# Last layer of a two-layer transformer on one core: half of the expert outputs kept on chip and turned by TensorE, half sent through DRAM as before

## The reference

```
grouped  = x.reshape(b, s // 32, 32, 256)               # groups n of 32 tokens: 128 in all
logits   = einsum('bntd,des->bntes', grouped, Wc) + bc   # 32 experts x 4 sets = 128 slots "es"
perm     = (logits + tie == max over the 32 tokens)      # one-hot: the token that slot es takes from group n
permuted = einsum('bntd,bntes->bnesd', grouped, perm)
inner    = relu(einsum('bnesd,esdf->bnesf', permuted, W1) + b1)    # f = 32 inner channels
result_p = einsum('bnesf,esdf->bnesd', inner, W2) + b2             # the second product
result   = einsum('bnesd,bntes->bntd', result_p, perm)             # back to the tokens
x        = x + result
```

## Time and profile before

| | us |
|---|---|
| median of three runs | 1857.89 |
| the profiled execution: its time | 1849.57 |
| the profiled execution: first to last instruction (span) | 1847.8 |
| TensorE busy | 1707.3 (92%) |
| VectorE busy | 1286.2 (70%) |
| ScalarE busy | 1145.3 (62%) |
| GpSimd busy | 821.8 (44%) |

### The profile page before, as it was taken

One profiled execution on the slowest core, in us unless ns is written; L12 is line 12 of the kernel. 1 busy time (PEld: TensorE's weight loads), 2 busy tenths in 40 slices (PEclk: granted clock), 3 DMA queues, 4 the chain that ended last, 5 costly groups with the idle time before them and its releaser, 6 DMA issues.

```text
span 1847.8 us, 41058 instructions
## 1 busy us (share of the span) xinstructions
PE 1707.3 (92%) x15760; PEld 1443.4 (78%) x15760; DVE 1286.2 (70%) x2770; ACT 1145.3 (62%) x2882; POOL 821.8 (44%) x1292
## 2 busy tenths in 40 slices
PE   5799999999999999999999789999999999988648
PEld 4567676679899999999999668888888888867523
DVE  4799998453518888888886687777777777667321
ACT  1477777423357777777775577777777777734210
POOL 2235442110103333333330677888888887644000
PEclk7799999999999999999999899999999999999766
DMA  7756565256966666666676522222223221112799
GB/s 185 212 125 137 131 128 130 72 181 223 317 232 223 242 242 240 242 243 240 244 237 239 193 71 64 69 88 72 66 64 92 70 64 54 43 49 94 267 365 325
DMA packets 140163, 303.81 MB, mean 164 GB/s; under 512 B 14080, under 2 KB 82944, under 8 KB 124736
## 3 DMA queue, kind: packets, MB, share of 16 engines
q1 hardware_dynamic: 116032, 188.68, 33.1%
q0 software_dynamic: 19584, 108.31, 17.2%
q10 hardware_dynamic: 4352, 4.20, 0.7%
HBM read 210.44 MB, written 90.44 MB: 163 GB/s over the span
## 4 chain that ended last, share of the span: by engine, by line
PE 74%; DVE 9%; DMA 7%; POOL 4%; issue 4%; ACT 1%; SPq 1%; DVEq 0%; POOLq 0%; ACTq 0%
PE ps L1250 12%; PE ps L1236 11%; PE ps L1832 5%; PE ps L373 5%; PE ps L219 4%; PE ps L1863 4%; PE ps L1818 4%; PE ps L1852 4%; PE ps L379 3%; PE ps L464 3%; PE ps L440 2%; DMA R<-rp_scratch 2%; DVE NM L592 2%; DMA rp_scratch<-RP 2%; POOL P L209 2%
## 5 line engine op out<-in xcount | busy, mean ns | idle before, releaser
L196 ACT ACTIVATE P<-ps,NM 128x256 f32<-128x256 f32 x512 | 236.2, 481 | 127.5 <-DVE NM L185 127.4
L209 POOL TENSOR_TENSOR P<-P,RS 128x1024 f32<-128x1024 f32 x128 | 242.9, 1903 | 72.5 <-DVE RS L203 72.0
L1236 PE MATMUL ps<-XRP,W1P 128*128 128x256 f32 x1872 | 226.8, 281 | 3.3 <-DVE W1P L1319 3.3
L1236 PEld LDWEIGHTS ps<-XRP,W1P 128*128 128x128 f32 x1872 | 220.1, 190 | 3.6 <-DVE W1P L1319 3.6
L1250 PE MATMUL ps<-W2P,HP 128*128 128x256 f32 x1872 | 221.5, 277 | 0.0
L1250 PEld LDWEIGHTS ps<-W2P,HP 128*128 128x128 f32 x1872 | 218.0, 188 | 0.0
L592 DVE TENSOR_REDUCE NM<-ps 128x2 f32<-128x512 f32 x256 | 164.3, 684 | 35.9 <-PE ps L440 35.1
L690 ACT ACTIVATE PT<-ps 128x512 f32<-128x512 f32 x256 | 139.2, 597 | 67.9 <-PE ps L452 65.4
L185 DVE TENSOR_REDUCE NM<-ps 128x2 f32<-128x512 f32 x256 | 164.5, 684 | 5.8 <-PE ps L1818 4.2
L1170 POOL DMA_INDIRECT WE<-in_we,WIX x39 | 44.6, 1144 | 268.9 <-DVE W1P L1319 208.8
L1279 ACT ACTIVATE HF<-ps,WE 128x256 f32<-128x256 f32 x312 | 129.0, 465 | 43.2 <-PE ps L1236 43.2
(11 more groups left out here) (225 smaller groups left out, 3688.7 us busy)
## 6 DMA issues: line engine op xcount, KB each, us to landing
KS<-k_scratch SPq DMA_DIRECT2D x64, 256.0 KB, 3.1
V<-v_scratch SPq DMA_DIRECT2D x16, 1024.0 KB, 6.3
rp_scratch<-RP SPq DMA_DIRECT2D x16, 1024.0 KB, 8.7
R<-rp_scratch SPq DMA_DIRECT2D x16, 1024.0 KB, 14.0
k_scratch<-KVM SPq DMA_DIRECT2D x52, 256.0 KB, 4.1
QS<-q_scratch SPq DMA_DIRECT2D x96, 128.0 KB, 4.5
v_scratch<-KVM SPq DMA_DIRECT2D x40, 256.0 KB, 3.0
ys_scratch<-YS SPq DMA_DIRECT2D x39, 256.0 KB, 8.1
```

The lines of the kernel that those rows point to most:

```text
L196: i = e.activation(self.P[u % 4][:, c, :], PS[SB[n % 3]][:, y * 256:y * 256 + 256], ACT.Exp, bias=self.NM[:, u % 4, c:c + 1], accum_out=se ...
L209: e.tensor_tensor(p, p, self.RS[:, u % 4, :].unsqueeze(2).to_broadcast([128, 4, 256]), ALU.mult).then_inc(self.s_pn, 1)
L1236: m = e.matmul(PS[p][:, hh * 256:hh * 256 + 256], W1P[i % 2][wi][:, cc * 1024 + hc * 128:cc * 1024 + hc * 128 + 128], XRP[i % 2][xi][:, cc ...
```

## The change

The 16 `down` steps become 8 pairs. `down_a(k)` is the second product for batches 0 to 7 (groups 0 to 63) and four experts: sixteen matmuls with 32 x 64 stationary and 256 columns moving. It is copied into `RPA` (two buffers) and goes through DRAM as before: 8 transfers of 1 MB, and 8 back. `down_b(k)` is the second product for batches 8 to 15 with the operands exchanged: the stationary operand is 32 x 128 of `WF2P`, the moving one 32 x 64 of `INT`, 32 matmuls for four experts. Channels are then on the partitions; DVE and ACT copy the banks into `RPB`, 64 KB per partition, in which the writes of one instruction are 512 bytes apart.

`turn_b(i)` turns `RPB` for one batch by 16 PE transposes into four banks, and DVE adds the bias `B2` while it moves them into `R2B` (two buffers). `back("b", ...)` needs no bias matmuls; `bias(b)` and `back("a", ...)` are the two parts of the former `back`. The returns alternate, b ahead of a (`RET`). Output transfers move from ACT's queue to SP's, in the order of `RET` and behind the `back_in` of the batch three later (`NR` = 3). `WF1P` has four buffers (6 loads in place of 8), `WF2P` four (no reuse), and the four parts of the first product in half 1 are made in the order 2, 3, 0, 1, ahead of all `down` steps.

```diff
-NR = 6
+NR = 3
+    R2A = [Arena(nc, q1_at + 8192 * i)(f"R2A{i}", [128, 8, 256], fp32) for i in range(NR)]
+    R2B = [Arena(nc, w1o_at + 8192 * i)(f"R2B{i}", [128, 8, 256], fp32) for i in range(2)]
+    RPA = [Arena(nc, ot1_at + 8192 * i)(f"RPA{i}", [128, 2, 4, 256], fp32) for i in range(2)]
+    RPB = Arena(nc, attn_at)("RPB", [128, 2, 64, 128], fp32)
+    PARTS = ((0, 1, 2, 3), (2, 3, 0, 1))
+    RET = [x for i in range(10) for x in ((("b", i - 1),) if 1 <= i <= 8 else ()) + ((("a", i - 2),) if i >= 2 else ())]
+    def rpa_free(w, k):
+        if k >= 2:
+            w.wait_ge(d_ks_rp[(k - 2) % 4], ks_sent + 16 * ((k - 2) // 4 + 1))
+    def rpb_part(k, r):
+        es = 16 * (4 * (k % 2) + k // 2) + r
+        return (RPB[:, :, :, :].rearrange("p a g s -> p s (a g)")[:, es:es + 13:4, :],
+                PS[GATHER[r]][:, :].rearrange("p (q n) -> p q n", q=4))
...
+        def down_a(k):
+            w.wait_ge(s_e0, 2 * k - 1)
+            w.wait_ge(s_e1, 2 * k - 1)
+            for h in range(2):
+                for a in range(2):
+                    for r in range(4):
+                        rows = slice(32 * r, 32 * r + 32)
+                        m = e.matmul(PS[SMALL[r]][64 * a:64 * a + 64, h * 256:h * 256 + 256],
+                                     INT[rows, 16 * a + 2 * k + h, 0:64],
+                                     WF2P[k // 2][rows, 4 * a + 2 * (k % 2) + h, :], start=True, stop=True)
+        def down_b(k):
+            w.wait_ge(s_in, 16)
+            w.wait_ge(s_e0, 2 * k)
+            w.wait_ge(s_e1, 2 * k)
+            for ql in range(4):
+                for dh in range(2):
+                    for r in range(4):
+                        rows = slice(32 * r, 32 * r + 32)
+                        c0 = (2 * ql + dh) * 64
+                        m = e.matmul(PS[GATHER[r]][:, c0:c0 + 64], WF2P[k // 2][rows, 4 * (k % 2) + ql, dh * 128:dh * 128 + 128],
+                                     INT[rows, 16 * (k % 2) + 4 * (k // 2) + ql, 64:128], start=True, stop=True)
+        def turn_b(i):
+            for t in range(4):
+                w.wait_ge(s_e0, 16 + 4 * (i - 1) + t + 1 if i else 16)
+                for u in range(2):
+                    for dh in range(2):
+                        c0 = u * 256 + dh * 128
+                        m = e.transpose(PS[SMALL[t]][:, c0:c0 + 128], RPB[:, dh, 8 * i + 2 * t + u, :], ident)
+                m.then_inc(s_fm, 1)
...
+        for x in range(4):
+            pe_up(e, w, 1, x)
+        for k in range(8):
+            down_a(k)
+            down_b(k)
+        for i in range(10):
+            if i < 8:
+                turn_b(i)
+            if i >= 2:
+                bias(i - 2)
+            if 1 <= i <= 8:
+                back("b", i - 1)
+            if i >= 2:
+                back("a", i - 2)
... dve_tail
+                for t in range(4):
+                    w.wait_ge(s_fm, 16 + 4 * i + t + 1)
+                    e.tensor_tensor(R2B[i % 2][:, 2 * t:2 * t + 2, :], PS[SMALL[t]][:, :].rearrange("p (n d) -> p n d", n=2),
+                                    B2[:, :].unsqueeze(1).to_broadcast([128, 2, 256]), ALU.add).then_inc(s_e0, 1)
... sp_tail
+        for j in range(4):
+            w.wait_ge(d_ks_rp[j], ks_sent + 16 * 2)
+        w.wait_ge(s_fm, 16)
+        for b in range(NR):
+            back_in(b)
+        for kind, b in RET:
+            if kind == "a" and b + NR < 8:
+                back_in(b + NR)
+            out(kind, b)
```

More of the change, by code:

```diff
@@ L81, in build @@
     vd = nc.dram_tensor("v_scratch", (16, 128, 2048), fp32).ap()
-    rpd = nc.dram_tensor("rp_scratch", (128, 128, 256), fp32).ap()
+    rpd = nc.dram_tensor("rp_scratch", (64, 128, 256), fp32).ap()
     X = keep("X", [128, 32, 256], fp32)
@@ L1475, in build @@
     WF2P = [Arena(nc, x3_at)("WF2P0", [128, 8, 256], fp32)]
+    XO = [Arena(nc, x3_at + 2048 * i)(f"XO{i}", [128, 2, 256], fp32) for i in range(4)]
     PMT = Arena(nc, w1q_at)("PMT", [128, 4096], f32r)
@@ L1478, in build @@
     X3P = [[mem_t(f"X3P{i}{j}", [128, 2, 256], f32r) for j in range(2)] for i in range(2)]
-    WF2P.append(Arena(nc, q1_at)("WF2P1", [128, 8, 256], fp32))
+    WF2P += [Arena(nc, q1_at + 8192 * i)(f"WF2P{i + 1}", [128, 8, 256], fp32) for i in range(3)]
+    R2A = [Arena(nc, q1_at + 8192 * i)(f"R2A{i}", [128, 8, 256], fp32) for i in range(NR)]
     WF1P = [mem_t(f"WF1P{i}", [128, 2, 32, 32], fp32) for i in range(2)]
@@ L1485, in build @@
     INT = Arena(nc, w1o_at)("INT", [128, 32, 128], fp32)
[L1486 to L1494, removed]
+    R2B = [Arena(nc, w1o_at + 8192 * i)(f"R2B{i}", [128, 8, 256], fp32) for i in range(2)]
+    WF1P += [Arena(nc, ot1_at + 8192 * i)(f"WF1P{i + 2}", [128, 2, 32, 32], fp32) for i in range(2)]
+    RPA = [Arena(nc, ot1_at + 8192 * i)(f"RPA{i}", [128, 2, 4, 256], fp32) for i in range(2)]
+    PX = Arena(nc, attn_at)("PX", [128, 2, 128, 64], fp32)
+    RPB = Arena(nc, attn_at)("RPB", [128, 2, 64, 128], fp32)
     d_c1 = sem("d_c1")
+    d_wf1, d_wf2 = [sem(f"d_wf1{i}") for i in range(2)], [sem(f"d_wf2{i}") for i in range(2)]
     wt_sent, kl_sent = 16, 16 * 32
@@ L1580, in pe_step, with pe_up @@
             gather(n - 3)
-    def pe_up(e, w, hf, j):
-        w.wait_ge(d_kl_wf1[j % 2], kl_sent + 16 * (2 * hf + j // 2 + 1))
+    def pe_up(e, w, hf, x):
+        j = PARTS[hf][x]
+        buf = j + 2 if hf and j < 2 else j % 2
+        if buf < 2:
+            w.wait_ge(d_kl_wf1[buf], kl_sent + 16 * (j // 2 + 1))
+        else:
+            w.wait_ge(d_wf1[j], 16)
         w.wait_ge(s_px, 24 * (hf + 1))
@@ L1588, in pe_up @@
                 for r in range(4):
-                    m = e.matmul(PS[GATHER[j]][32 * r:32 * r + 32, q * 64:q * 64 + 64], WF1P[j % 2][:, cc, 4 * q + r, :],
+                    m = e.matmul(PS[GATHER[j]][32 * r:32 * r + 32, q * 64:q * 64 + 64], WF1P[buf][:, cc, 4 * q + r, :],
                                  PX[:, cc, 32 * j + 4 * q + r, :], start=(cc == 0), stop=(cc == 1))
@@ L1593, in pe_tail, with second_in @@
     def pe_tail(e, w):
-        def down(q2):
-            w.wait_ge(d_wt_wf2[q2 // 4 % 2], wt_sent + 16 * (q2 // 8 + 1))
-            w.wait_ge(s_in, 8 + 2 * (q2 // 4) + 2)
+        def second_in(j):
+            if j < 2:
+                w.wait_ge(d_wt_wf2[j], wt_sent + 16)
+            else:
+                w.wait_ge(d_wf2[j - 2], 16)
+        def down_a(k):
+            second_in(k // 2)
+            w.wait_ge(s_in, 8)
             w.wait_ge(s_rb, 32)
@@ L1600, in down @@
             w.wait_ge(s_pb, 16)
[L1601 to L1608, removed]
@@ L1628, in back @@
-            m.then_inc(s_cm2, 1)
[L1630 to L1637, removed]
+                    e.matmul(M[:, lt * 256:lt * 256 + 256], PMT[:, tok + lt * 128:tok + lt * 128 + 128], B2S[j][:, :],
+                             start=(lt == 0 and j == 0), stop=(j == 1), skip_group_check=True)
+        def back(kind, b):
+            n = returned(kind, b)
+            M, tok = PS[GATHER[(n - 1) % 4]], 256 * (b + 8 * (kind == "b"))
+            if kind == "a":
+                R = R2A[b % NR]
+                w.wait_ge(d_r2[b % NR], 16 * (b // NR + 1))
+            else:
+                R = R2B[b % 2]
+                w.wait_ge(s_e0, 16 + 4 * b + 4)
+                w.wait_ge(s_xo, n - 4)
+            for lt in range(2):
+                for g in range(4):
+                    c0 = tok + lt * 128 + 32 * g
+                    m = e.matmul(M[32 * g:32 * g + 32, lt * 256:lt * 256 + 256], PMT[:, c0:c0 + 32].bitcast(fp32),
+                                 R[:, 2 * g + lt, :], start=(kind == "b" and lt == 0), stop=True, skip_group_check=True)
+            m.then_inc(s_cm2, 1)
@@ L1705, in dve_up, with r2b_free @@
         e.tensor_scalar(INT[:, 8 * j:8 * j + 8, hf * 64:hf * 64 + 64], RL[:, :, :], 0.0, None, ALU.max).then_inc(s_in, 1)
[L1707 to L1712, removed]
-    def dve_tail(e, w):
[L1715 to L1719, removed]
+    def r2b_free(w, i):
+        if i >= 2:
+            w.wait_ge(s_cm2, returned("b", i - 2))
@@ new lines, in dve_tail, with out_add @@
+    def dve_tail(e, w):
+        def out_add(kind, b):
+            n = returned(kind, b)
+            t, m = 2 * (b + 8 * (kind == "b")), (n - 1) % 4
+            w.wait_ge(s_cm2, n)
+            w.wait_ge(d_x_wf2_out[m], 16 + 16 * ((n - 1) // 4))
+            e.tensor_tensor(flat(XO[m][:, :, :]), flat(X[:, t:t + 2, :]), PS[GATHER[m]][:, :], ALU.add).then_inc(s_xo, 1)
+        for x in range(4):
+            dve_up(e, w, 1, x)
+        for k in range(8):
+            w.wait_ge(s_fm, 2 * k + 1)
+            rpa_free(w, k)
@@ L1720, in dve_tail @@
             for r in range(2):
-                i = e.tensor_copy(RP[out_at(q2)][:, :, r, :], PS[DOWN[down_set(q2)][r]][:, :].rearrange("p (q d) -> p q d", q=2))
+                i = e.tensor_copy(*rpa_part(k, r))
             i.then_inc(s_e0, 1)
[L1723 to L1728, removed]
+            w.wait_ge(s_fm, 2 * k + 2)
@@ new lines, in dve_tail @@
+            for r in range(2):
```

(73 more changed lines are left out.)

41 lines of the change are left out of this document (15 added, 26 removed).

## The result

The changed kernel took 1944.34 us, the median of four runs (1941.75 to 1951.48), against 1857.0 us before on the same chip: a ratio of 1.0478, 95% interval 1.0447 to 1.0509. It is 87 us slower where 37 us faster was forecast. The profiled execution took 1944.29 us, with a span of 1942.4.

What follows compares the result with a forecast made beforehand. DMA transfers were taken as the bound from 1740 us. First product to 1731, second to 1757.0, returns 50.5, end 3.4: span 1810.9, 36.9 less; from 1857.89 that gives 1821 us (0.50), range 1811 to 1832.

Steps and rivals of the forecast that it cites:

- first product of half 1: 512 matmuls, all four parts ahead of the second product, no load waits: ends at 1731 us (1729.9 to 1732.1).
- The step that failed: Second product, `RPA` with two buffers: 3.1 us per k, eight k 24.8 us, ending at 1757.0 us.
- the change doesn't relieve the transfers: Rival: writes of `down_a` come out as slow as sixteen; then about 1857 us; chance 0.02.
- The wait that the sum names: Second product: a copy into an `RPA` buffer waits for the transfer of k-2; two k take 1.30 + 0.37 + landing.
- `down_b`'s loads: Second product: 32 weight loads of 32 x 128, 0.037 us apart, 1.2 us per `down_b`, 1.3 with the fill.
- the rival in which each costs its own duration: `down_b` weight loads don't overlap: 5.9 us at 0.185 each, all gain gone; 1896 us at 0.333; chance 0.06.
- The copies into `RPB`: Second product: strided copies take 0.68 us like those into `PX`, making DVE's floor 2.7 us per k.
- The bound of twice that: Upper bound on `RPB` copy time, twice 0.68 us; it would add 22 us.
- The clock: Second product at full level; returns with one 24 us low spell, 50.5 us. Rivals: full 1812 (0.22), low 1841 (0.20).
- The rule that I had weighed: Returns: a transpose doesn't count as busy as a matmul does, so doesn't bring the full clock; would give the low-clock sum.
- The returns: After the second product: 5.0 us per batch pair at full clock, 8.9 at low; eight pairs 40 or 71 us.
- outer range of 1806 to 1843: From the full-clock case with shorter second product upward; some 0.15 of the chance is left out of it.

Runs made afterwards that it cites:

- with two writes: Changed kernel with each 1 MB write of `RPA` to the scratch issued as two of 0.5 MB (partitions 0 to 63, 64 to 127): 1836.63 us, ratio to before 0.9899.

## Why the prediction was wrong, point by point

| from the first matmul of half 1, us | forecast | changed kernel | with two writes |
|---|---|---|---|
| first product of half 1 | 15.0 | 19.5 | 17.2 |
| second product (to the first transpose) | 26.0 | 125.9 | 49.2 |
| returns and end | 53.9 | 76.4 | 43.1 |
| sum | 94.9 | 221.7 | 109.6 |

(The 76.4 of the changed kernel hold a wait of 32 us for the last write and the first read, the rest of the same cause. The times by stage are those of one profiled execution.)

**The step that failed** is in the second product: "two k take 1.30 + 0.37 + landing. The shortest landing was 3.9", hence "I take 3.1" us per k. It priced a new transfer by the bytes and run length of the old one. Its shape had changed, and by the runs above that alone is worth 107 us, 1944.3 to 1836.6: 37.8 us a landing, two at a time, is 18.9 us per k. No rival held it. The one nearest, that the change doesn't relieve the transfers, took sixteen fast writes as the worst case. The wait that the sum names, a copy behind the write of k-2, was the right one; the landing in it came out seven to ten times as long as the 5.5 and 3.9 us that I took.

**`down_b`'s loads.** "32 are 1.2 us, 1.3 with the fill": it is 64 instructions, 2.0 us at the full clock. They do overlap, 0.031 us apart, so the mechanism was right and its count was half; the rival in which each costs its own duration, 0.185, did not occur. `down_a` is 32 instructions as well, not 16, but takes 1.05 us at the full clock, so its 1.19 held.

**The copies into `RPB`.** "I take 0.68 for `RPB` too": 1.03 in the changed kernel's median, 1.33 with two writes. The bound of twice that held, but its price was wrong: sixteen copies by 0.68 more are 10.9 us, not 22. The nearest row did not carry over; `PX` is written in pairs. The Trainium skill, page "SBUF — State Buffer", section "Specifications (TRN2)", asks for two hits per 16-byte line for the full rate; 0.68 for pairs, 0.68 for whole runs and 1.03 to 1.33 for single elements agree with it. Why the last comes at two values no run shows.

**The clock** came out the other way round. I took the full level for the second product, by a window in which `down` stood there, and one low spell for the returns. With two writes the second product stands at 0.50 from its third k on and the returns at 1.00. The clock rose while PE did nothing but transposes (line 1652 from 1791.46 to 1797.66; the granted clock is 0.50 to 1796 and 1.00 from 1797). The changed kernel shows it alone: PE idle for 15.7 us, then transposes only from 1865.99 to 1871.55, 0.50 up to 1869 and 0.84 over the next 3 us. So in these traces the clock did rise on transposes. The rule that I had weighed, of the Trainium skill's page "TensorE: Matmul & The Clock Gate", section "PE-mode transpose", disagrees with these traces, and the measurement decides.

**The returns** were over-priced: 4.24 us a pair at the full clock (1798.66 to 1802.90) where I had 5.0, since pieces that I had read one by one overlap (bias 0.47 for the four in place of 1.0, returns 1.86 in place of 2.28). DVE lay beside PE as forecast. Outputs did make DVE wait for a free `XO`, which I had put at nothing: 5.8 us in four waits with two writes. Two landings of 8.58 and 6.55 us stand in its chain, whose last 24 us run through the outputs, with PE still at work beside them up to about 1830; they are in the 43.1 us.

**What held:** transfers bounded the kernel before; the change with half their bytes pays about 1% once they run on all engines; the returns then fill PE and the DMA engines together (1.03 share). With that one edit the time, 1836.6, is within the outer range of 1806 to 1843, but above the forecast's own (1811 to 1832) and 15.6 above the forecast. That nearness is in part luck, as terms of opposite sign cancel: 23 us too little for the second product, 11 too much for returns and end, 2 too little for the first product (its chain has three gaps, 2.14, 1.19 and 3.14 us, where I had one and a half of 2.18).

## What to carry to other kernels

Price a transfer by its access pattern too, not by its bytes alone: check the outermost dimension on both sides, and keep it a multiple of 16 (the share stood at 0.95 and more with 16 and 128, and at 0.13 and 0.25 with 2 and 4), by splitting the transfer or by a layout whose rows merge. In a profile the sign is a DMA share that stands at a round fraction of sixteen (0.13, 0.25) while something waits for the transfer. Count instructions in the trace, not calls in the program, before a load or matmul rate is multiplied.

## What the runs showed that I had not expected

Two reads of 64 partitions in place of one of 128 were slower: 248 GB/s at a DMA share of 1.13 over 20 us of the returns (1804 to 1824), against 336 GB/s at 1.03 with two writes and undivided reads. Group strides in DRAM differ as well between the two (64 KB against 128 KB), so the cause stays open.

Two levels of the clock were seen for PE work of the same density, by what else was in the mix, as told above. And the layers ahead of the change differ between executions: the first product of half 1 began between 1714.6 and 1723.8 us in the four profiled executions with the old tail and between 1720.7 and 1737.3 us in those with the new one. Part of that can be the change's (the earlier `WF1P` loads, an engine's work falling in step with another's); I did not test it.
